# Moving the feed-forward layers and the spike comparisons to other steps of a fused attention kernel

## What is computed

```
xn = layernorm(x)
h  = layernorm(xn) * ln_scale + ln_bias
q, k, v = up-projections of h @ w_down_q.T and h @ w_down_kv.T; rotary embedding on q and k
attn = softmax(q k^T / sqrt(64));  a = (attn v) @ w_out.T + xn
y = square(relu(xn @ W_fc.T)) @ W_proj.T          # 128 -> 512 -> 128
5 times: mem = 0.9 * mem + y - reset; spike = mem > 1
out = x + a + (number of spikes) / 5
```

## Time and profile before

| | |
|---|---|
| median of 3 runs | 1110.21 us (1109.39 to 1112.67) |
| profiled execution, device time | 1110.22 us |
| its span, first to last instruction | 1108.4 us |
| granted TensorE clock, mean | 0.995 |
| TensorE matmul busy | 1050.3 us (95%) |
| VectorE busy | 908.6 us (82%) |
| ScalarE busy | 930.4 us (84%) |
| GpSimd busy | 894.9 us (81%) |
| DMA queue of the kernel, share of 16 engines | 73.6% |

### The profile page before, as it was taken

How to read it: one execution, slowest core, us unless ns; L and a number is a source line. 1 busy time by engine, 2 the same in 40 slices (tenths; PEclk the granted TensorE clock), 3 DMA queues, 4 the chain that set the end, 5 groups by cost and what they waited for, 6 DMA issues and landing times.

```text
span 1108.4 us, 26191 instructions
## 1 busy us (share of the span) xinstructions
PE 1050.3 (95%) x6880; PEld 711.4 (64%) x6880; DVE 908.6 (82%) x1223; ACT 930.4 (84%) x3136; POOL 894.9 (81%) x897
## 2 busy tenths in 40 slices
PE   3789999999999999999999999999999999999987
PEld 3556666666666666666666666666666666666654
DVE  3788888888888888888888888888888888888872
ACT  3789888888888888988888888888888888898871
POOL 3677888888888888888888888888888898888861
PEclk9899999999999999999999999999999999999999
DMA  5287768777777877777877777877777787777773
GB/s 181 89 216 210 200 187 218 205 204 196 200 201 200 218 201 196 203 202 195 229 197 192 212 195 194 221 203 204 199 199 202 200 218 201 196 200 202 189 199 92
DMA packets 93281, 217.96 MB, mean 197 GB/s; under 512 B 22464, under 2 KB 43200, under 8 KB 93120
## 3 DMA queue, kind: packets, MB, share of 16 engines
q1 hardware_dynamic: 92864, 216.52, 73.6%
q10 hardware_dynamic: 384, 1.05, 0.4%
HBM read 7.77 MB, written 4.19 MB: 11 GB/s over the span
## 4 chain that ended last, share of the span: by engine, by line
PE 48%; DVE 15%; ACT 14%; issue 13%; SPq 6%; DMA 2%; DVEq 1%; ACTq 1%; POOL 0%; POOLq 0%
PE ps_s L328 12%; PE ps_u L342 12%; PE ps_b L447 10%; ACT prob L538 7%; DVE neg_max L688 6%; SPq L254 5%; PE ps_a L383 5%; PE ps_qk L318 4%; PE ps_qk L319 2%; DVE turned L699 2%; DVE latent L727 2%; DVE qk L683 2%; DMA gathered<-turned 2%; ACT raw L550 2%; ACT spread L562 2%
## 5 line engine op out<-in xcount | busy, mean ns | idle before, releaser
L538 ACT ACTIVATE prob<-ps_s,neg_max 128x256 f32<-128x256 f32 x1024 | 473.8, 484 | 93.8 <-DVE neg_max L688 93.0
L833 POOL TENSOR_TENSOR partner<-partner,rope_sb 128x512 f32<-128x512 f32 x256 | 326.7, 1276 | 137.1 <-DMA partner<-raw 134.6
L688 DVE TENSOR_REDUCE neg_max<-ps_s 128x4 f32<-128x1024 f32 x256 | 309.9, 1211 | 101.8 <-PE ps_s L328 100.7
L836 POOL TENSOR_TENSOR qk<-qk,partner 128x512 f32<-128x512 f32 x256 | 326.3, 1275 | 20.1
L699 DVE STREAM_TRANSPOSE turned<-prob 128x1024 f32<-128x1024 f32 x256 | 315.3, 1232 | 1.2 <-ACT prob L538 0.2
L328 PE MATMUL ps_s<-qk 64*128 64x256 f32 x2048 | 292.7, 405 | 3.4 <-ACT prob L538 2.4
L342 PE MATMUL ps_u<-gathered,ckv 128*64 128x256 f32 x2048 | 277.5, 392 | 7.0 <-DMA gathered<-turned 5.5
L328 PEld LDWEIGHTS ps_s<-qk 64*128 64x128 f32 x2048 | 177.8, 187 | 112.3 <-issue 92.1
L538 ACT ACTIVATION_READ_ACCUMULATOR prob<-ps_s,neg_max 128x1 f32 x1024 | 220.2, 215 | 0.0
L683 DVE TENSOR_TENSOR qk<-ps_qk,rope_sb 128x512 f32<-128x512 f32 x256 | 175.0, 684 | 41.7 <-ACT raw L550 34.9
L550 ACT COPY raw<-ps_qk 128x512 f32<-128x512 f32 x256 | 155.2, 606 | 48.9 <-PE ps_qk L319 48.5
(11 more groups left out here) (67 smaller groups left out, 909.2 us busy)
## 6 DMA issues: line engine op xcount, KB each, us to landing
gathered<-turned SPq DMA_DIRECT2D x1016, 128.0 KB, 2.4
partner<-raw SPq DMA_DIRECT2D x256, 256.0 KB, 2.4
x_sb<-in_x SPq DMA_DIRECT2D x32, 128.0 KB, 2.2
resid<-early SPq DMA_DIRECT2D x32, 128.0 KB, 2.0
out<-out_sb SPq DMA_DIRECT2D x32, 128.0 KB, 2.0
turned<-in_wup SPq DMA_DIRECT2D x2, 512.0 KB, 5.7
gathered<-turned ACTq DMA_DIRECT2D x8, 128.0 KB, 4.4
rope_sb<-in_rope SPq DMA_DIRECT2D x1, 512.0 KB, 6.8
```

Source lines behind the costliest of these rows:

```text
L538: last = nc.scalar.activation(prob[:, s % 2, :, h, :, t, :].rearrange("p j k c -> p k j c"), ps_s[:, s % 2, h, t, :].rearrange("p (k j c) ...
L688: nc.vector.tensor_reduce(neg_max[:, s % 2, :, :], ps_s[:, s % 2, :, :, :], AXIS_X, ALU.max, negate=True).then_inc(max_ready, 1)
L833: nc.gpsimd.tensor_tensor(other, other, sin_sb, ALU.mult).then_inc(sin_ready, 1)
L836: nc.gpsimd.tensor_tensor(qk[:, s % 4, :, :], qk[:, s % 4, :, :], other, ALU.add).then_inc(rope_done, 1)
```

## The change

Steps are numbered 0 to 7 here; in the words "steps 3 and 4" of a count from 1 they would be 2 and 3.

- The first feed-forward layer of batch b + 1 moves from steps 5 and 6 to steps 2 and 3, on TensorE and (its rectification) on ScalarE. The squares stay in steps 6 and 7.
- The second layer of batch b moves from steps 2 and 3 to steps 4 and 5. Since the next batch's rectified values are written before it has read its own, `relu_sb` gets two buffers.
- The five comparisons move from steps 3 and 4 to step 6, all together behind the step's transpose.
- The input transposes of step 7 and the latents by token of step 0 wait for the comparisons (`lif`) where they waited for the rectification (`relu_done`); the first layer no longer waits for the comparisons.
- The broadcasts of the inverse sums stand ahead of the feed-forward products in a step. On ScalarE the copies of the spread sums of steps 1 to 3 stand ahead of the exponentials, that of step 0 ahead of the latent copies, and with it the copy of the weighed latents of step 0.
- The transposes of the finished sum and of the inverse sums (step 7) stand behind the weighing instead of ahead of it.
- In the last batch, three groups of the last attention output come together in step 7.

```diff
-        relu_sb = sb("relu_sb", [P, FC, S])
+        relu_sb = sb("relu_sb", [P, 2, FC, S])
...
 (transpose_inputs)
-                pe.wait_ge(relu_done, done(2 * (n - 2) + 1))
+                if not outside(n - 3, B):
+                    pe.wait_ge(lif, done((n - 3) * LIF_OPS + LIF_OPS - 1))
...
 (latents_by_token)
-                pe.wait_ge(relu_done, done(2 * (n - 1) + 1))
+                if not outside(n - 2, B):
+                    pe.wait_ge(lif, done((n - 2) * LIF_OPS + LIF_OPS - 1))
...
 (ffn_in)
                 if half == 0:
-                    pe.wait_ge(lif, done((n - 1) * LIF_OPS + LIF_OPS - 1))
                     if not outside(n + 1, B):
                         pe.wait_ge(latent_split, done(n + 1))
                     pe.wait_ge(ckv_ready, done(n))
                 else:
                     pe.wait_ge(relu_done, done(2 * n))
...
-            def ffn_out(n, half):
-                if half == 0:
-                    if not outside(n + 2, B):
-                        pe.wait_ge(latent_split, done(n + 2))
-                    elif not outside(n + 1, B):
-                        pe.wait_ge(ckv_ready, done(n + 1))
+            def ffn_out(n, half, par):
+                if half == 0 and not outside(n + 1, B):
+                    pe.wait_ge(relu_done, done(2 * (n + 1) + 1))
...
 (extras)
-                    elif p == 6:
-                        last_attention_out(b, 0, b0)
-                        last_attention_out(b, 1, b0)
                     elif p == 7:
-                        last_attention_out(b, 2, b0)
+                        for c in range(3):
+                            last_attention_out(b, c, b0)
...
-                if not outside(b, B) and p in (2, 3):
-                    ffn_out(b, p - 2)
-                if not outside(b + 1, B) and p in (5, 6):
-                    ffn_in(b + 1, p - 5, 1 - b0)
                 if p < 4 and not outside(b - 1, LAST):
                     broadcast_rden(b - 1, p)
+                if not outside(b + 1, B) and p in (2, 3):
+                    ffn_in(b + 1, p - 2, 1 - b0)
+                if not outside(b, B) and p in (4, 5):
+                    ffn_out(b, p - 4, b0)
                 if p == 7:
                     if not outside(b + 3, B):
                         transpose_inputs(b + 3, 1 - b0)
-                    if not outside(b - 1, B):
-                        transpose_sum(b - 1)
-                    if not outside(b, LAST):
-                        transpose_rden(b)
...
 (TensorE's step)
                 if not outside(g, STEPS):
                     weigh_latents(g, s, i)
+                if p == 7 and not outside(b - 1, B):
+                    transpose_sum(b - 1)
+                if p == 7 and not outside(b, LAST):
+                    transpose_rden(b)
...
-            def relu(n, half):
+            def relu(n, half, par):
                 act.wait_ge(fc_ready, done(2 * n + half))
+                act.wait_ge(y_ready, done(n - 2))
...
 (ScalarE's step)
+                if p in (1, 2, 3) and not outside(b - 1, LAST):
+                    copy_spread(b - 1, p)
                 if not outside(g + LEAD["scores"], STEPS):
                     exponentials(g + LEAD["scores"], s + LEAD["scores"], i)
+                if p == 0 and not outside(g, STEPS):
+                    copy_u(g, s, i)
+                if p == 0 and not outside(b - 1, LAST):
+                    copy_spread(b - 1, 0)
...
-                if not outside(b + 1, B) and p in (5, 6):
-                    relu(b + 1, p - 5)
+                if not outside(b + 1, B) and p in (2, 3):
+                    relu(b + 1, p - 2, 1 - b0)
...
-                if p < 4 and not outside(b - 1, LAST):
-                    copy_spread(b - 1, p)
-                if not outside(g, STEPS):
+                if p > 0 and not outside(g, STEPS):
                     copy_u(g, s, i)
...
 (VectorE's step)
-                    if p == 3:
-                        for k in (0, 1):
+                    if p == 6:
+                        for k in range(LIF_OPS):
                             integrate(b, b0, k)
                     elif p == 4:
-                        for k in (2, 3, 4):
-                            integrate(b, b0, k)
```

More of the change, by code:

```diff
@@ L395, in ffn_out @@
                     c = 2 * half + j
-                    last = nc.tensor.matmul(ps_a[:, 0:S], wproj_sb[:, c, :], relu_sb[:, c, :],
+                    last = nc.tensor.matmul(ps_a[:, 0:S], wproj_sb[:, c, :], relu_sb[:, par, c, :],
                                             start=(c == 0), stop=(c == FC - 1))
@@ L562, in copy_spread, with square @@
                 nc.scalar.copy(spread[:, c % 2, :, :], ps_b[:, :].rearrange("p (j s) -> p j s", j=2)).then_inc(bc_evac, 1)
-            def square(n, half):
+            def square(n, half, par):
                 act.wait_ge(relu_done, done(2 * n + half))
                 c = slice(2 * half, 2 * half + 2)
-                nc.scalar.activation(relu_sb[:, c, :], relu_sb[:, c, :], ACT.Square).then_inc(sq_done, 1)
+                nc.scalar.activation(relu_sb[:, par, c, :], relu_sb[:, par, c, :], ACT.Square).then_inc(sq_done, 1)
             def normalise(n, par, which):
@@ L599, in copy_latents @@
                     .then_inc(ckv_ready, 1)
-            def relu(n, half):
+            def relu(n, half, par):
                 act.wait_ge(fc_ready, done(2 * n + half))
-                nc.scalar.activation(relu_sb[:, 2 * half:2 * half + 2, :],
+                act.wait_ge(y_ready, done(n - 2))
+                nc.scalar.activation(relu_sb[:, par, 2 * half:2 * half + 2, :],
                                      ps_a[:, :].rearrange("p (c s) -> p c s", c=2), ACT.Relu).then_inc(relu_done, 1)
@@ L665, in step @@
                         copy_inputs(b + 3, 1 - b0)
-                if p < 4 and not outside(b - 1, LAST):
-                    copy_spread(b - 1, p)
-                if not outside(g, STEPS):
+                if p > 0 and not outside(g, STEPS):
                     copy_u(g, s, i)
                 if p in (6, 7) and not outside(b + 1, B):
-                    square(b + 1, p - 6)
+                    square(b + 1, p - 6, 1 - b0)
                 if is_last(b) and p < 2:
```

## The result

| | before | after |
|---|---|---|
| median | 1110.43 us (1109.39 to 1112.67, 4 runs) | 1131.44 us (1130.50 to 1132.65, 4 runs) |
| ratio, 95% interval | | 1.0186 (1.0170 to 1.0202) |
| span of the profiled execution | 1108.4 us | 1130.1 us |

What follows compares the result with a forecast made beforehand. The prediction took TensorE's own order of work as the limit, with 1.52 us of waiting a batch. Its terms summed to +0.66 us a batch, +19 us over about 29 batches, +1 in the last: 1130 us, range 1098 to 1144.

Steps and rivals of the forecast that it cites:

- step 0, backlog of ScalarE: Broadcast of step 0 wanted before the late copy of the inverse sums ends: +0.28 us a batch, bounds 0 and 0.5.
- step 1, wait removed less backlog: In step 1 the wait for the spread copy goes, -0.55 us; the broadcast waits for step 0's spread copy, +0.13.
- step 3, first layer waits: In step 3 the first layer's second half waits for the first rectification, late behind exponentials: +0.95 us, upper bound 1.2.
- steps 4 to 6, wait removed: Step 4's wait on a spread copy goes, -0.34 us a batch; the moved layers add no wait there.
- step 7: removed, change of shape, new wait: Spike-term wait gone, -0.63 us; one more tile-shape change, +0.17; input transposes wait for the five comparisons, +0.65.
- ends of the program: In the last batch two final attention products move from step 6 into step 7, behind the comparisons: +1 us.
- The new waits: Input transposes on the comparisons in step 7, 0.65 us; first layer on the rectification in step 3, 0.9 us.
- both waits are hidden: Rival: VectorE and ScalarE run far enough ahead, leaving only -1.35 us a batch: 1071 us, chance 0.10.
- there is no backlog: Rival: only waits from order stay, comparisons 0.65 and rectification 0.5 us; -0.20 a batch, 1104 us, chance 0.18.
- the second rival: Only the waits that follow from order stay, with no backlog on ScalarE: 1104 us, chance 0.18.
- the backlog reaches on to steps 2 to 4: Rival: weighing or second layer there also waits for ScalarE, or all terms at upper bounds: +1.1 us, 1142, chance 0.12.
- the waits only change names: Rival: what is freed in steps 1, 4 and 7 is lost in 3 and 7: within 0.3% of 1110, chance 0.12.

## Why the prediction was right

It said slower, 1130 us from 1098 to 1144, own range 1120 to 1139. Measured 1131.4. Against its own terms, in us per batch:

| term | predicted | measured | read from |
|---|---|---|---|
| step 0, backlog of ScalarE | +0.28 | +0.25 | mean of step 0; broadcast 2.66 against 2.41 |
| step 1, wait removed less backlog | -0.42 | -0.45 | mean of step 1 |
| step 3, first layer waits | +0.95 | +0.89 | mean of step 3; gone with the early rectification |
| steps 4 to 6, wait removed | -0.34 | -0.33 | means of the three, 12.56 against 12.89 |
| step 7: removed, change of shape, new wait | -0.63 + 0.17 + 0.65 = +0.19 | -0.48 + 0.17 + 0.45 = +0.14 | mean of step 7; parts from four kernels |
| batch | +0.66 | +0.50 | mean of 24 batches |
| ends of the program | +1 | about +6 | below |

*The new waits.* Both came with the names foretold, 26 and 30 times where I had said about 29. The rectification ends where the sum of durations put it: forecast 9.56 us after step 1's start as TensorE sees it, measured 9.59 (532.47 to 542.06). That is the term which decides the sign, and the early rectification took 20 us away with it alone. The sum itself gave a wait of 0.88; I had raised it to 0.95, and 0.89 was measured. The step lengths foretold (4.8, 4.5, 3.6, 5.1) were measured as 4.75, 4.48, 3.60 and 5.08.

*Step 7.* Two terms were mis-sized and nearly cancel. "Four transposes take 0.42 us" was read from the second group, which stands behind other transposes; the input transposes stand behind an attention product and take about 0.16 more, the difference of the brackets 0.33 and 0.17. The kernels without any wait in step 7 show it (4.63 to 4.64). So the wait removed was 0.48 where I had 0.63, and the new one by the same measure is 0.45 (5.08 less 4.63) where I had 0.65. That the step came out right (+0.14 for +0.19) is luck.

*The change of shape.* I took 0.17, the bracket in the trace behind transposes, over the full 0.38. The run with one change added measured 0.15 in step 7. The rule of the Trainium skill (page "TensorEngine Tiling (Array Packing)", section Tiling Modes) is that changing the tiling mode drains TensorE. The traces agree that each change has an idle stretch ahead of the next load. They add that its length differs: 0.38 to 0.39 behind a weighing, 0.33 behind an attention product, 0.17 behind transposes, and 0.14 behind the broadcast of the inverse sums (522.38 to 522.52 in the trace before). What sets the length is not shown. The width of the matmuls alone does not, since those of the broadcast have 256 columns like those of the product. One cannot count changes at a flat price.

*The removed waits on spread copies.* -0.55 and -0.34 came true by luck, since they need a condition that the prediction did not have. It costed this part at 0.89 us a batch, 26 us; alone it gives nothing, because step 4's weighing waits for transfers next. In the earlier trace rows nothing waits for them, but the view of waits had them 19 times (11.2 us), and the prediction put them at nothing without a reason. With the second layer in step 4 they are covered, and there the part is worth 19 us. Two parts that were summed as independent are not.

*The sum.* 0.50 a batch instead of 0.66, so some 14.5 us instead of 19 over 29 batches, and the rest, some 6.5, at the ends instead of 1. I gave the last batch 1 us for two attention products. Its second layer moved too, out of the steps where TensorE waits, and after a stretch of little work the granted clock was 0.50 for 5 us. The two errors are near 5 us each and cancel, so that the total is nearer than its parts by luck. Of the ends, 3.1 us lie behind the last score load. What makes the other 3, at the start (1.4) and in the last batches, stays open.

*The rivals.* That both waits are hidden (1071) and that there is no backlog (1104) are refuted by the trace after. With four comparisons left out the kernel comes out at 1103.6, near the second rival's time but by another way: the wait of step 3 is there (23.7 us) and that of step 7 is gone. That the backlog reaches on to steps 2 to 4 was not seen: step 2 is 3.84 and step 4 is 4.48, as foretold. That the waits only change names (1110) is refuted by the time.

## What to carry to other kernels

Where the order on each engine is fixed, price a move by following the moved instruction's queue: what stands ahead of it there, when that ends, and who on the bounding engine asks for it first; here that gave the largest wait to 0.06 us, and one move inside ScalarE's queue was worth 20 us. A wait that is taken away is worth only what the next latest thing leaves, so look for transfers that land about when the engine arrives, before the gain is added up. Work that waits for nothing, such as a feed-forward layer here, can stand ahead of a wait and cover it. What its move takes away has to be looked at in the last round too, when nothing else is left to fill the engine.

## What was not expected of the hardware

- A second queue did not help where the DMA engines were nearly full: with two of sixteen transfers on ScalarE's queue the engines read 0.97 busy at 204 GB/s, after 0.91 at 208 GB/s with one queue, a transfer took 3.6 to 4.5 us from issue to landing instead of 2.4, and the kernel lost 26 us.
- SyncE's issue takes the same 0.62 us for a transfer of 128 KB and for one of a quarter of that (eight in 5.00, four in 2.49).
- The idle bracket at a change of tile shape is not one number: 0.14 us behind the broadcast, 0.17 behind transposes, 0.33 behind an attention product, 0.38 to 0.39 behind a weighing. A wait of the next load that ends inside it adds nothing.
- Late in the program TensorE's granted clock fell to 0.50 for about 5 us, after 3 us of which the engine was busy 0.97; with 1.74 busy in the same stretch it stayed at 1.00. Eight weighing matmuls took 1.98 us at 0.50 instead of 1.08 at 1.00.
